# A two-layer block with a state-space scan: router steps moved to ScalarE, projections, an x tile and a turn of y moved in TensorE's order

## What is computed

```python
x, gate = proj[..., :1024], proj[..., 1024:]            # h @ W_in.T
x = silu(conv_b + sum(conv_w[:, j] * xpad[:, j:j+L, :] for j in range(4)))
ts, Bm, Cm = split(x @ W_x.T)                            # each then rms-normed
dt = softplus(ts @ W_dt.T + b_dt)
state = state * exp(dt * A) + (dt * u) * B               # step by step along the tokens
y = einsum('bdn,bn->bd', state, C)
y = (y + x * D) * silu(gate);  x1 = x0 + ga * (y @ W_out.T)

base = h @ base_W.T
probs = softmax(h @ router_W.T);  top_vals, top_idx = top_k(probs, 2)
rw = top_vals / sum(top_vals)                            # shares of the two experts
w_dense = sum(one_hot(top_idx, 8) * rw)
inc = einsum('bser,erd->bsd', einsum('bsd,edr->bser', h, lora_A) * w_dense, lora_B)
out = x1 + gb * (base + inc * 2)
```

## Time and profile before

| what | value |
|---|---|
| median of 3 runs | 1551.36 us (1547.93 to 1553.31) |
| profiled execution | 1553.72 us, of which the span is 1551.9 |
| granted TensorE clock, mean | 0.955 of full speed |
| VectorE busy | 1241.2 us, 80% of the span |
| GpSimd busy | 1037.3 us, 67% |
| ScalarE busy | 936.9 us, 60% |
| TensorE busy, products | 1386.7 us, 89% |
| VectorE's scans, L2242 | 512 of 1267 ns, 626.8 us |
| GpSimd's dt*u*B, L2054 | 256 of 2357 ns, 598.1 us |
| ScalarE's exponentials, L1732 | 1024 of 466 ns, 443.0 us |

### The profile page before, as it was taken

How to read it: one execution, slowest core, us unless ns; L and a number is a source line. 1 busy time by engine, 2 the same in 40 slices (tenths; PEclk the granted TensorE clock), 3 DMA queues, 4 the chain that set the end, 5 groups by cost and what they waited for, 6 DMA issues and landing times.

```text
span 1551.9 us, 25257 instructions
## 1 busy us (share of the span) xinstructions
PE 1386.7 (89%) x8817; PEld 998.1 (64%) x8817; DVE 1241.2 (80%) x1634; ACT 936.9 (60%) x2548; POOL 1037.3 (67%) x731
## 2 busy tenths in 40 slices
PE   6779999999999869699899899899899999988677
PEld 5457677767776657567667667667666756755543
DVE  4684764556443479999999999999999999999993
ACT  3342343233321587878787787787787787786751
POOL 0343242313223297897997998898898898899870
PEclk9699999999999989899999999999999999999688
DMA  9431222101100200200110110110020020020001
GB/s 328 161 121 47 82 82 82 55 28 35 35 28 33 69 14 1 81 2 15 56 41 15 55 42 1 55 56 1 15 96 1 15 94 4 1 69 28 1 1 41
DMA packets 32388, 77.16 MB, mean 50 GB/s; under 512 B 3667, under 2 KB 4723, under 8 KB 31750
## 3 DMA queue, kind: packets, MB, share of 16 engines
q1 hardware_dynamic: 32262, 75.55, 14.5%
HBM read 66.99 MB, written 8.55 MB: 49 GB/s over the span
## 4 chain that ended last, share of the span: by engine, by line
POOL 24%; PE 24%; DVE 10%; issue 7%; ACT 3%; DVEq 0%; POOLq 0%; ACTq 0%
POOL dbu L2054 14%; POOL h L2089 7%; PE ps_h L1486 6%; DVE h L2242 5%; DVE acc L2258 3%; PE ps_m L1450 3%; PE ps_o L1510 2%; PE ps_m L165 2%; PE ps_s L1450 2%; PE ps_m L166 1%; PE ps_m L167 1%; ACT ps_a L1732 1%; POOL dtu L2170 1%; POOL dt L2134 1%; PE ps_h L1471 1%
## 5 line engine op out<-in xcount | busy, mean ns | idle before, releaser
L2242 DVE TENSOR_TENSOR_SCAN h<-ps_a,carry,dbu 128x512 f32<-128x512 f32 x512 | 626.8, 1267 | 14.6 <-ACT ps_a L1732 5.0
L2054 POOL TENSOR_TENSOR dbu<-dtu,b_all 128x1020 f32<-128x1020 f32 x256 | 598.1, 2357 | 18.8 <-DVE h L2242 18.8
L1732 ACT ACTIVATE ps_a<-dt,a_neg 128x256 f32<-128x256 f32 (+1 forms) x1024 | 443.0, 466 | 118.9 <-DVE h L2242 118.5
L1486 PE MATMUL ps_h<-ident,h 128*128 128x128 f32 x1536 | 231.3, 294 | 70.0 <-DVE acc L2258 66.0
L2258 DVE SCALAR_TENSOR_TENSOR acc<-ps_h,c_cur,acc 128x512 f32<-128x512 f32 x384 | 268.9, 740 | 21.2 <-PE ps_h L1486 20.1
L1486 PEld LDWEIGHTS ps_h<-ident,h 128*128 128x128 f32 x1536 | 184.0, 150 | 126.9 <-DVE h L2242 84.0
L714 POOL TENSOR_TENSOR hid_l<-hid,hid_h 128x256 f16<-128x256 f32 (+1 forms) x88 | 77.0, 878 | 159.1 <-ACT hid_h L605 159.0
L2089 POOL TENSOR_TENSOR h<-h,c_all 128x1024 f32<-128x1024 f32 x64 | 151.0, 2359 | 22.1 <-ACT carry L1752 22.1
L597 ACT ACTIVATE sil<-ps_gu 128x256 f32<-128x256 f32 (+1 forms) x88 | 34.0, 386 | 180.2 <-PE ps_gu L167 180.2
L165 PE MATMUL ps_m<-h_h,wi_h 128*128 128x256 f16 x432 | 120.7, 279 | 4.1 <-PEq L155 2.4
L166 PE MATMUL ps_m<-h_l,wi_h 128*128 128x256 f16 x432 | 120.1, 278 | 0.0
(11 more groups left out here) (399 smaller groups left out, 2864.0 us busy)
## 6 DMA issues: line engine op xcount, KB each, us to landing
b_all<-bt_scratch SPq DMA_DIRECT2D x32, 512.0 KB, 3.8
wm<-in_wmod SPq DMA_DIRECT2D x7, 1024.0 KB, 5.2
wo<-in_wmod SPq DMA_DIRECT2D x5, 1024.0 KB, 8.3
xa<-in_x SPq DMA_DIRECT2D x8, 512.0 KB, 4.4
stage<-in_W_in SPq DMA_DIRECT2D x4, 1024.0 KB
x_scratch<-x SPq DMA_DIRECT2D x8, 512.0 KB, 3.1
c_all<-bt_scratch SPq DMA_DIRECT2D x8, 512.0 KB, 6.3
x<-x_scratch SPq DMA_DIRECT2D x8, 512.0 KB, 3.6
```

Of the source, the lines that this page charges most:

```text
L1486: tr = pe.transpose(ps_h[:, t, j * P:(j + 1) * P], h[:, s % RING, j, t * P:(t + 1) * P], W["ident"][:])
L1732: ex = nc.scalar.activation(ps_a[:, j, j % 2:], dt[:, m, j % 2:], ACT.Exp, scale=a_neg[:, m, st:st + 1])
L2054: nc.gpsimd.tensor_tensor(dbu[:, s % AHEAD, :, 1:], dtu[:, :, 1:], b_all[:, st, 1:].unsqueeze(1).to_broadcast([P, DG, CH - 1]), ALU.mult). ...
L2242: nc.vector.tensor_tensor_scan(h[:, s % RING, two].rearrange("p j t -> p (j t)"), ps_a[:, two].rearrange("p j t -> p (j t)"), dbu[:, s % A ...
```

## The change

There are four parts.

1. Router. On GpSimd the subtraction of the two logits, the sum 1 + e, the power and the product go. ScalarE makes e from the logits (Exp with a scale of -1 and the other logit as bias, one column for each half of the tokens), then ln(1 + e), exp of its negative, and the product, all after the table load of slot 23, which has both Exp and Ln. In the last chunk's iteration, which had no such load, one is added. After the last chunk GpSimd has no router work; DVE converts the indices, compares, and makes the shares with a reciprocal.
2. Projection behind the first turned state. Piece 5 moves from slot 5 to slot 6, behind `turn_h` of the fourth slot's state; `turn_h` of slot 5's state stands between pieces 5 and 6. Where p is None, the turn stays where it was. In slot 7 the turn of that slot's own state comes before piece 7. In slots 22 and 23 the same is done with the first piece of the experts: it moves from the end of slot 23 to the end of slot 22.
3. First x tile. It moves from slot 6 to slot 7 (`FIRST_X`), so slot 7 has tiles 0 and 1.
4. y. `turn_y(i, 2)` comes after `wx` instead of before it, and `make_y(i, 2)` on DVE one slot later, in slot 19.

The diff, cut to its core:

```diff
@@ -59,12 +59,13 @@
 T3_AT = {3: (0,), 4: (1,)}
-WO_AT = {0: (1,), 1: (2,), 3: (3,), 4: (4,), 5: (5,), 6: (6,), 7: (7,)}
+WO_AT = {0: (1,), 1: (2,), 3: (3,), 4: (4,), 6: (5, 6), 7: (7,)}
 WO_NEXT = {30: (0,)}
...
 XT_AT = {6 + m: (m,) for m in range(KI)}
+FIRST_X = 7
 T4_AT = {12: (0,), 14: (1,)}
-YA_AT = {16: (0,), 17: (2,)}
+YA_AT = {16: (0,), 18: (2,)}
 RA_AT = 17
@@ -1618,9 +1618,15 @@
                     add_h(i, KC - 1, first)
+                if s == FIRST_X:
+                    if n is not None:
+                        x_tile(n, 0, False)
+                    turn_h(i, s)
                 if p is not None and s:
...
                         out_projection(p, q)
+                        if q == 5:
+                            turn_h(i, s - 1)
                 if p is not None and s == RA_AT:
@@ -1629,10 +1635,12 @@
                     add_h(i, NS, first)
-                for m in YA_AT.get(s, ()):
-                    turn_y(i, m)
-                if n is not None and s == WX_AT:
-                    wx(n)
+                if s == NS:
+                    turn_y(i, 0)
+                if s == WX_AT:
+                    if n is not None:
+                        wx(n)
+                    turn_y(i, 2)
                 if n is not None and s == WX_AT + 1:
@@ -1642,7 +1650,8 @@
                     for m in XT_AT.get(s, ()):
-                        x_tile(n, m, False)
+                        if m:
+                            x_tile(n, m, False)
                 if p is not None and s == (MID_LAST if n is None else MID_AT):
@@ -1661,12 +1670,12 @@
                     init_acc(i, s // NS)
-                if st == JOIN_AT + 1:
+                if st == JOIN_AT + 1 and (p is None or s > NS):
                     turn_h(i, s - 1)
-                if st == JOIN_AT + 2:
+                if p is not None and n is not None and s == NS + JOIN_AT + 1:
+                    experts(p, 0)
+                if st == JOIN_AT + 2 and s != FIRST_X:
                     turn_h(i, s)
-                if p is not None and n is not None and s == NS + JOIN_AT + 2:
-                    experts(p, 0)
@@ -1885,8 +1894,21 @@
         def router_exp(p):
-            act.wait_ge(S["gap_done"], p + 1)
-            nc.scalar.activation(e2[:], gap[:], ACT.Exp).then_inc(S["e2_done"], 1)
+            act.wait_ge(S["top_done"], p * TT + TT)
+            for t in range(TT):
+                op = nc.scalar.activation(e2[:, t:t + 1], top[:, t, 0:1], ACT.Exp, scale=-1.0, bias=top[:, t, 1:2])
+            op.then_inc(S["e2_done"], 1)
+        def router_share(p):
+            act.wait_ge(S["e2_done"], p * 4 + 1)
+            nc.scalar.activation(e2p[:], e2[:], ACT.Ln, bias=1.0).then_inc(S["e2_done"], 1)
+            act.wait_ge(S["e2_done"], p * 4 + 2)
+            nc.scalar.activation(w12[:, 0], e2p[:], ACT.Exp, scale=-1.0).then_inc(S["e2_done"], 1)
+            act.wait_ge(S["e2_done"], p * 4 + 3)
+            for t in range(TT):
+                op = nc.scalar.activation(w12[:, 1, t:t + 1], e2[:, t:t + 1], ACT.Copy, scale=w12[:, 0, t:t + 1])
+            op.then_inc(S["e2_done"], 1)
@@ -1973,6 +1995,9 @@
                     nc.scalar.preload_act_table_set("natural_log_exp_and_others")
+                    if p is not None:
+                        router_exp(p)
+                        router_share(p)
                 if s == 25:
@@ -1983,8 +2008,10 @@
                     nc.scalar.preload_act_table_set("exp_and_others")
-            if p is not None and s == RA_AT + 5:
+            if p is not None and n is None and s == 23:
+                nc.scalar.preload_act_table_set("natural_log_exp_and_others")
                 router_exp(p)
+                router_share(p)
             if p is not None and s == MID_AT:
@@ -2133,32 +2160,22 @@
-        def gap_of(p):
+        def chosen(p):
             pool.wait_ge(S["top_at_done"], p * TT + TT)
-            nc.gpsimd.tensor_tensor(gap[:], top[:, :, 1], top[:, :, 0], ALU.subtract).then_inc(S["gap_done"], 1)
-            nc.gpsimd.tensor_copy(at[:], top_at[:, :, 0:2]).then_inc(S["at_done"], 1)
-        def weigh(p, last=False):
-            pool.wait_ge(S["e2_done"], p + 1)
+            nc.gpsimd.tensor_copy(at[:], top_at[:, :, 0:2]).then_inc(S["weigh_step"], 1)
+        def weigh(p):
+            pool.wait_ge(S["weigh_step"], p * 6 + 1)
+            pool.wait_ge(S["e2_done"], p * 4 + 4)
             pool.sem_inc(W["met_pool"], 1)
-            nc.gpsimd.tensor_scalar(e2p[:], e2[:], 1.0, None, ALU.add).then_inc(S["weigh_step"], 1)
-            pool.wait_ge(S["weigh_step"], p * 8 + 1)
-            nc.gpsimd.tensor_tensor(w12[:, :, 0], e2p[:], W["mhalf"][:, 3 * TT:3 * TT + TT], ALU.pow).then_inc(S["weigh_step"], 1)
-            pool.wait_ge(S["weigh_step"], p * 8 + 2)
-            nc.gpsimd.tensor_tensor(w12[:, :, 1], w12[:, :, 0], e2[:], ALU.mult).then_inc(S["weigh_step"], 1)
-            if last:
-                return
-            pool.wait_ge(S["weigh_step"], p * 8 + 3)
-            pool.wait_ge(S["at_done"], p + 1)
-            pool.sem_inc(W["met_pool"], 1)
             for t in range(TT):
                 for b in range(2):
-                    nc.gpsimd.tensor_scalar(wd[:, b, t], expert[:], at[:, t, b:b + 1], w12[:, t, b:b + 1],
+                    nc.gpsimd.tensor_scalar(wd[:, b, t], expert[:], at[:, t, b:b + 1], w12[:, b, t:t + 1],
                                             ALU.is_equal, ALU.mult).then_inc(S["weigh_step"], 1)
-            pool.wait_ge(S["weigh_step"], p * 8 + 7)
+            pool.wait_ge(S["weigh_step"], p * 6 + 5)
             nc.gpsimd.tensor_tensor(wd[:, 0], wd[:, 0], wd[:, 1], ALU.add).then_inc(S["weigh_step"], 1)
-            pool.wait_ge(S["weigh_step"], p * 8 + 8)
+            pool.wait_ge(S["weigh_step"], p * 6 + 6)
             nc.gpsimd.tensor_tensor(mid.rearrange("p t (e r) -> p t e r", e=NE),
@@ -2180,7 +2197,7 @@
             if p is not None and s == RA_AT + 6:
-                gap_of(p)
+                chosen(p)
             if p is not None and s == RA_AT + 9:
@@ -2219,8 +2236,6 @@
             inv_std_last(t)
-        gap_of(LASTC)
-        weigh(LASTC, True)
@@ -2318,16 +2333,26 @@
-            dve.wait_ge(S["weigh_step"], LASTC * 8 + 3)
-            dve.wait_ge(S["at_done"], NCH)
+            done = LASTC * 6
+            dve.wait_ge(S["top_at_done"], NCH * TT)
+            nc.vector.tensor_copy(at[:], top_at[:, :, 0:2]).then_inc(S["weigh_step"], 1)
+            dve.wait_ge(S["weigh_step"], done + 1)
             dve.sem_inc(W["met_dve"], 1)
...
                 for b in range(2):
-                    nc.vector.tensor_scalar(wd[:, b, t], expert[:], at[:, t, b:b + 1], w12[:, t, b:b + 1],
-                                            ALU.is_equal, ALU.mult).then_inc(S["weigh_step"], 1)
-            dve.wait_ge(S["weigh_step"], LASTC * 8 + 7)
+                    nc.vector.tensor_scalar(wd[:, b, t], expert[:], at[:, t, b:b + 1], None, ALU.is_equal).then_inc(S["weigh_step"], 1)
+            dve.wait_ge(S["e2_done"], LASTC * 4 + 1)
+            nc.vector.tensor_scalar(e2p[:], e2[:], 1.0, None, ALU.add).then_inc(S["weigh_step"], 1)
+            dve.wait_ge(S["weigh_step"], done + 6)
+            nc.vector.reciprocal(w12[:, 0], e2p[:]).then_inc(S["weigh_step"], 1)
+            dve.wait_ge(S["weigh_step"], done + 7)
+            nc.vector.tensor_tensor(w12[:, 1], w12[:, 0], e2[:], ALU.mult).then_inc(S["weigh_step"], 1)
+            dve.wait_ge(S["weigh_step"], done + 8)
+            nc.vector.tensor_tensor(wd[:], wd[:], w12[:].unsqueeze(3).to_broadcast([P, 2, TT, NE]), ALU.mult)\
+              .then_inc(S["weigh_step"], 1)
+            dve.wait_ge(S["weigh_step"], done + 9)
             nc.vector.tensor_tensor(wd[:, 0], wd[:, 0], wd[:, 1], ALU.add).then_inc(S["weigh_step"], 1)
-            dve.wait_ge(S["weigh_step"], LASTC * 8 + 8)
+            dve.wait_ge(S["weigh_step"], done + 10)
             nc.vector.tensor_tensor(mid.rearrange("p t (e r) -> p t e r", e=NE),
...
                                     wd[:, 0].unsqueeze(3).to_broadcast([P, TT, NE, LORA]), ALU.mult).then_inc(S["mid_done"], 1)
```

5 lines of the change are left out of this document (2 added, 3 removed).

## The result

| what | before | after |
|---|---|---|
| median | 1548.11 us (12 runs, 1542.08 to 1553.31) | 1538.99 us (12 runs, 1534.71 to 1541.29) |
| ratio, 95% interval | | 0.9935 [0.9921, 0.995] |
| profiled execution (span) | 1553.72 us (1551.9) | 1540.32 us (1538.5) |
| granted clock, mean | 0.955 | 0.954 |
| chunk, fifth | 122.46 us | 120.19 us |

On the 1551.36 us from which the forecast started the ratio gives 1541.3, a gain of 10.1 us; forecast were 1540.7 and 10.7. In the changed kernel the helper lines have moved: the scan is L2257, VectorE's add L2273, GpSimd's product L2081 and weighted state L2116, ScalarE's exponentials L1741; turned states (L1486), additions (L1471) and projections (L1510) kept theirs.

A forecast was written before the change was run, and what follows sets the result against it. GpSimd's back-to-back part and TensorE's part were taken to bound each chunk. 1.38 + 0.51 = 1.9 us per pass, seven passes with shorter ends, gave 10.7 us off 1551.36: 1540.7 us, range 1535 to 1547.5.

The forecast's parts named there:

- What bounds the kernel: Steady chunk: only shortening GpSimd's or TensorE's part counts; VectorE's 4.20 us of waits are symptoms.
- a ring: GpSimd's back-to-back work from slot 16 to next slot 6 (75.92 us), then TensorE's to slot 16 (46.82 us).
- Router and experts: Slots 22 to 29: router leaving GpSimd saves 1.54 us, alone only 0.8; with experts' products moved, GpSimd gains 1.46.
- The clock in slot 23: Products filling TensorE's gap keep its clock up at slot 23's transposes; VectorE gains 0.66 us, 0 if it falls.
- Slots 5 to 8: TensorE starts adding the fourth state 1.38 us earlier; its run to the first convolution drops 0.51 to 14.26 us.
- The early stalls partly return in slots 12 to 16: VectorE runs ahead after slot 6 and waits later, in slots 12 to 16, for tanh and x tiles.
- W_x before the turn of y: Slot 20's 0.50 us wait mostly goes, worth nothing; VectorE waits about 0.3 us before slot 23's scan instead.
- ScalarE's six operations: After slot 23's table load: six small operations take 1.5 us, free within 2.7 us of room; at 3.0 cost 0.3.
- The first chunk's −0.3: First chunk, no router: moved x tile sits behind a VectorE wait where the clock may fall; loss 0.3 us, 0 to 1.
- Given back: Rival, chance 0.15: GpSimd's lead is lost at scan waits, stalls return in slots 12 to 16; 3 us gain, 1548.4.
- slower: Rival, chance 0.05: TensorE's clock falls in slots 6 to 8, cancelling the 1.9 us per pass; 1556 us at worst.
- More falls: Rival, chance 0.10: waits for tanh and y go too, 2.8 us per pass, 1535 us.

The follow-up runs named there:

- each of the kernels above: The kernels before and after, and variants with one part undone, one part alone, filled gaps or further reorderings; steady chunks 119.53 to 122.73 us.
- the old order: Changed kernel with the experts' first products back at the end of slot 23: steady chunk 120.18 to 120.83 us, ratio 0.994.
- the other reorderings tried: Changed kernel with later softplus sum and earlier first turn of y: 120.17 us; changed kernel with halved projections plus tanh before the next x tile: 119.53 us.

## Why the prediction was right, and where not

**What bounds the kernel.** Right. Two parts of a ring, GpSimd's and TensorE's, add up to the chunk in each of the kernels above, and a change in one leaves the other within 0.3 us of its length. The experts' move alone, which takes 0.65 us off VectorE's waits in slot 23 (0.46 before the first half, the rest before the second) and gives back 0.64 in slot 6, shows it most plainly.

**Router and experts.** Right in both sizes: 0.75 for the router alone with the clock low (forecast 0.8), 1.40 for both (forecast 1.38 for the start of the addition, 1.46 for GpSimd). The softplus sum is 1.43 us nearer to slot 16, as GpSimd's list gave it. VectorE waits 0.16 in slot 23, as taken. In the working the 1.46 does not follow from its own numbers: 1139.02 less the 1137.5 set down for the logarithm is 1.5.

**The clock in slot 23.** The number was right and the reason only half. The clock did not stay up. In five of six chunks it falls as in the kernel before, but in slots 22, 24 or 25, where VectorE's timeline has no wait for it. And with the old order it does not strike slot 23's transposes each time, only in three chunks of six. So the term was 0.64 in some chunks of the old order and not a fixed 0.66. The trace of the kernel before has the signs of it: VectorE waits 0.61 us in slot 23 in the second to fifth chunk, but 0.42 in the sixth and 0.15 in the seventh, and the prediction read only the fifth.
The Trainium skill (TensorE: Matmul & The Clock Gate, Part 4: PE-mode transpose) would have transposes not count as activity. Here ten of them in the gap served as well as six products, one execution of six chunks each. If transposes did not count, about half of the chunks should have taken 120.8 us, as three of six did with nothing in the gap, and none did. The measurement decides for this kernel; with six chunks it is no proof against the rule.

**Slots 5 to 8.** The run to the first convolution was forecast at 14.26 us and is 14.21. What the step missed lies behind it. TensorE's part fell by 0.85 in all and not by 0.51. Before the change an x tile waited 0.18 us in slot 9 until VectorE had emptied its bank, and the first two steps from convolution to convolution took 4.28 and 4.48 us; now VectorE is no longer late there and both take 4.23. The sum stopped at the convolution and should have gone on to slot 16. That makes 2.2 us a pass instead of 1.9. "The early stalls partly return in slots 12 to 16" held: 0.33 and 0.34 for tanh. Also wrong in the working: TensorE's readiness for the addition was worked out "without the fifth projection in slot 5", but that piece stands behind the addition in the old order too and cannot delay it, and undoing the move left the addition where it was (GpSimd's part 74.56). The near tie of GpSimd and TensorE was right all the same: with GpSimd's state 0.14 us earlier the addition came only 0.02 us earlier. And the x tile was costed as harmless for ScalarE only (it waits 2.29 us for it, with nothing lost, as forecast); that its old place is worth 0.6 us was not seen.

**W_x before the turn of y.** Right that it is worth nothing, wrong on where the wait goes. Forecast was 0.3 us before slot 23's scan; it stands before slot 21's (0.44), for TensorE's late addition.

**ScalarE's six operations.** Right: forecast 1.5 us, measured 1.47, hidden. The exponentials' table is ready 1.29 us after its load begins. The Trainium skill (ScalarE: Activation LUTs, What ACT_TABLE_LOAD costs) has a drain besides, 2.66 us in all; these rows show none.

**The ends and the sum.** Five steady passes and the one without router before them give (121.64 − 120.19) + (612.16 − 600.92) = 12.7 us in the profiled pair, where 0.4 + 9.5 were forecast. The last pass, forecast at 1.1, gave nothing that can be seen: from its start to the end of the span it was 152.7 us before and 153.1 after. Its slot 6 wait went as said, and at slot 22's scan VectorE is 1.55 us ahead of the kernel before, counted from the chunk's start. Then it waits 2.11 us for TensorE where 1.11 stood. TensorE in slots 21 and 22 of the last chunk, before and after:

```profile
1478.84 1.09 PE L1471 MATMUL ps_h<-ident,h 128*128 128x128 f32 x8 [1.80 <-POOL h L2089]
1480.34 1.49 PE L1486 MATMUL ps_h<-ident,h 128*128 128x128 f32 x8 [0.40 <-ACT acc L1911]
```
```profile
1464.13 1.09 PE L1471 MATMUL ps_h<-ident,h 128*128 128x128 f32 x8 [1.79 <-POOL h L2116]
1465.62 1.83 PE L1486 MATMUL ps_h<-ident,h 128*128 128x128 f32 x8 [0.40 <-ACT acc L1933]
```

From the chunk's start (1399.19 and 1385.37) the addition is only 0.89 us earlier, since it waits for GpSimd's state in both, and the turned state behind it takes 1.83 us instead of 1.49. That leaves 0.55 us at slot 23's scan and 0.2 at the end of the scans. What takes this rest behind the scans stays open. The first chunk's −0.3 did not show either (124.87 and 124.77). In the runs the gain is 10.1 us, 7.8 to 12.3 by the interval. So that the total came out nearly right is in part luck: steady passes that won more met a last pass that won nothing, and the ends of the program vary by several us from kernel to kernel. Why the runs give less than the chunks is not settled beyond that.

**The rivals.** "Given back" and "slower" fall: TensorE's clock is 1.00 from slot 6 to 16. "More falls" fails for the waits it named; of the 2.8 us a pass it would need, 2.2 came.

## What to carry to other kernels

In a ring of engines a wait tells where the later part arrives, not where the time is lost: cut the cycle where one engine runs without rest, give each stretch its length, and only what shortens one of them counts. Price a saving together with what is late right behind it, since the experts' move is worth 0 alone and 0.65 behind the router's where the low clock strikes. Compare repeated stretches of a trace where the total varies: in the changed kernel they agree to 0.02 us, while layer 1's start differs by 6 us between kernels. Look for work that can be cut to the size of a gap: half a piece of projection in a gap of 0.66 us, and another half moved forward, were worth 0.56 us a chunk, more than the other reorderings tried (0, and 0.09 on top of it).

## What was not expected of the hardware

- The lower clock comes about once a chunk, and its place shifts: in slot 23 in all six chunks of the kernel before, in slots 22, 24 or 25 in five of six after the change. It costs nothing unless an engine waits for TensorE there (0.64 us a chunk if VectorE does).
- With about 1.3 us of further work in slot 22 and the experts' products still in slot 23, it came in one chunk of six instead of five, and transposes did this as well as products (one execution of each).
- The last chunk has the clock low for long: in the profiled execution after the change the granted clock was 0.50 from about 1421 to 1452 us, with TensorE busy for 19.7 of 30.7 us.
